# A graph network's edge rows: more of them fetched row by row by SyncE and ScalarE, fewer by GpSimd's gathers

## The reference

```python
x_src = x[src]; x_dst = x[dst]
e = relu((x_dst - x_src) @ theta_w.T + theta_b + x_src @ phi_w.T + phi_b)
x = layernorm(x + segment_max(e, dst))            # 0 for nodes without edges
hv = x @ W_in + b_in
for W, b in ((W_u0, b_u0), (W_u1, b_u1)):
    m = relu(concatenate([hv[src], edge_attr_64]) @ W + b)
    hv = where(has_in, segment_max(m, dst) + hv, hv)
x = layernorm(x + relu(hv @ W_ro + b_ro))
```

## Time and profile before

| | |
|---|---|
| device time, median of 3 runs | 4386.74 us |
| lowest and highest of the 3 | 4368.79 and 4420.99 us |
| span of the profiled execution (first to last instruction) | 3216.1 us |
| TensorE's mean granted clock in it | 0.922 |

### The profile page before, as it was taken

One profiled execution on the slowest core, in us unless ns is written; L12 is line 12 of the kernel. 1 busy time (PEld: TensorE's weight loads), 2 busy tenths in 40 slices (PEclk: granted clock), 3 DMA queues, 4 the chain that ended last, 5 costly groups with the idle time before them and its releaser, 6 DMA issues.

```text
span 3216.1 us, 33579 instructions
## 1 busy us (share of the span) xinstructions
PE 2494.2 (78%) x6386; PEld 1183.3 (37%) x6386; DVE 1457.3 (45%) x3424; ACT 196.1 (6%) x439; POOL 2359.0 (73%) x2484
## 2 busy tenths in 40 slices
PE   8776666666676888887887888688888888888877
PEld 6432222222223533333333333353333344333335
DVE  2675556555556533333433334323333343333337
ACT  2000000000002400000000000010000000000005
POOL 5777777777776677777777777667777777777765
PEclk9898888788877999999999999899999999999989
DMA  7666667666665777777777777687777777777764
GB/s 263 232 223 222 225 224 268 221 224 214 211 210 191 246 242 244 245 244 244 245 252 246 245 244 247 207 271 249 250 251 252 252 267 247 253 249 252 250 210 153
DMA packets 266593, 762.66 MB, mean 237 GB/s; under 512 B 57652, under 2 KB 113823, under 8 KB 229903
## 3 DMA queue, kind: packets, MB, share of 16 engines
q0 software_dynamic: 118896, 324.63, 33.2%
q1 hardware_dynamic: 94110, 356.95, 28.8%
q10 hardware_dynamic: 53376, 78.93, 7.9%
HBM read 413.88 MB, written 346.41 MB: 236 GB/s over the span
## 4 chain that ended last, share of the span: by engine, by line
POOL 39%; PE 17%; DMA 16%; issue 16%; SPq 7%; DVE 2%; ACT 2%; DVEq 0%; ACTq 0%; POOLq 0%
POOL gath L606 38%; DMA gath<-table,src_sb 14%; PE edge_ps L887 6%; SPq L530 4%; PE edge_ps L885 3%; PE edge_ps L778 3%; SPq L526 2%; PE side_ps L778 2%; PE edge_ps L864 2%; POOL gath L633 1%; DVE hist L410 1%; ACT x_sb L718 1%; DMA runs<-hist 1%; SPq L529 1%; DMA table<-hist 1%
## 5 line engine op out<-in xcount | busy, mean ns | idle before, releaser
L606 POOL DMA_INDIRECT gath<-table,src_sb x2288 | 2165.4, 946 | 745.0 <-issue 649.6
L410 DVE SCALAR_TENSOR_TENSOR hist<-hist,lift,edge_ps 128x256 f32<-128x256 f32 x2346 | 1127.0, 480 | 1564.3 <-PE edge_ps L887 1142.8
L887 PE MATMUL edge_ps<-gath,ident 128*128 128x512 f32 x1548 | 842.6, 627 | 328.0 <-DMA gath<-table,src_sb 326.4
L885 PE MATMUL edge_ps<-w_e,he_sb 128*128 128x512 f32 x1564 | 813.9, 602 | 5.5 <-DMA he_sb<-in_he 5.0
L864 PE MATMUL edge_ps<-gath,ident 128*128 128x512 f32 x740 | 476.3, 767 | 269.9 <-DMA gath<-table,src_sb 164.2
L887 PEld LDWEIGHTS edge_ps<-gath,ident 128*128 128x128 f32 x1548 | 275.7, 193 | 803.9 <-DMA gath<-table,src_sb 595.9
L885 PEld LDWEIGHTS edge_ps<-w_e,he_sb 128*128 128x128 f32 x1564 | 295.4, 194 | 352.7 <-issue 335.0
L864 PEld LDWEIGHTS edge_ps<-gath,ident 128*128 128x128 f32 x740 | 155.5, 236 | 532.5 <-DVE hist L410 317.1
L676 ACT COPY hv_sb<-side_ps 128x256 f32<-128x256 f32 x147 | 54.8, 373 | 2770.2 <-PE edge_ps L887 1842.9
L633 POOL DMA_INDIRECT gath<-runs,end_row x147 | 152.1, 1035 | 49.0 <-issue 43.6
L786 PE MATMUL edge_ps<-dst_f,onehot 128*128 128x512 f32 x200 | 78.0, 514 | 14.2 <-DVE onehot L333 14.2
(11 more groups left out here) (137 smaller groups left out, 1070.6 us busy)
## 6 DMA issues: line engine op xcount, KB each, us to landing
runs<-hist SPq DMA_DIRECT2D x285, 1024.0 KB, 5.0
he_sb<-in_he ACTq DMA_DIRECT2D x194, 256.0 KB, 2.9
late_sb<-table SPq DMA_DIRECT2D x3072, 1.0 KB
gath<-table,src_sb POOLq DMA_INDIRECT x2288, 3.4
table<-hist SPq DMA_DIRECT2D x72, 256.0 KB, 3.4
back_T<-x1T ACTq DMA_DIRECT2D x98, 128.0 KB, 3.2
runs<-hist SPq DMA_DIRECT2D x33, 256.0 KB, 2.9
x_sb<-in_x SPq DMA_DIRECT2D x49, 128.0 KB, 2.8
```

The costliest lines, as they stand in the source:

```text
L410: state = V.scalar_tensor_tensor(hist[:, s % H, :], hist[:, (s - 1) % H, :], lift[:, t:t + 1], edges, ALU.add, ALU.max)
L606: pool.indirect_dma_start(gath[:, s % G, :], None, a["x"] if s < RAW else tables[r], bass.IndirectOffsetOnAxis(src_sb[:, t:t + 1], 0)).the ...
L885: T.matmul(bank, he_sb[:, c % NHE, at:at + P], w_e[r - 1][:, :], start=True, stop=False)
L887: last = T.matmul(bank, ident[:, :], flat(edge_rows(s)), start=False, stop=True)
```

## The change

The number of row-by-row steps goes from 8 to 24 a round. SP fetches seven pairs of steps (first steps 120, 222, ..., 732): 14 steps, 1792 rows a round in place of 1024, 20 rows in each of the chunks 0 to 89. ACT fetches five pairs (first steps 148, 276, ..., 660): ten steps, 1280 rows a round, 16 rows in each of the chunks 0 to 79. POOL skips these 24 steps. The row numbers are multiplied by 1024 once, by DVE in the setup (12 small instructions), and written to `late_list` in HBM by one DMA after the 13th table write; the copies take the registers as byte offsets, so the instruction that computed an address falls away. [...] SP's destination is double buffered. ACT's is `he_sb` in round 0 (which is not in use there) and a part of `query_sb` afterwards, which joins the former `dst_f` and `junk`.

```diff
-LATE_AT = (360, 720)
-LATE = 4
-LATE_ROWS = 16
+LATE = 2
+LATE_PAIRS = 7
+LATE_EVERY, LATE_FIRST = 102, 120
+LATE_BUFS = 2
+LATE_PER_CHUNK = 20
+SIDE_PAIRS = 5
+SIDE_EVERY, SIDE_FIRST = 128, 148
+SIDE_PER_HALF_TURN = 16
+LATE_LOAD = 16
+ROW_BYTES = 4 * D
...
         def by_pool(t):
-            return t < STEPS and late_group(t) is None
+            return t < STEPS and late_pair(t) is None and side_pair(t) is None
...
             dve.wait_ge(edges_loaded, 16 * len(edge_loads))
+            firsts = [late_step(n) for n in range(LATE_PAIRS)] + [side_step(n) for n in range(SIDE_PAIRS)]
+            for n, first in enumerate(firsts):
+                last = V.tensor_scalar(late_at[:, n, :], src_sb[:, first:first + LATE], ROW_BYTES, None, ALU.mult)
+            reached("late offsets", last)
...
             def late_rows(r, c):
...
+                total = LATE_PAIRS * P * LATE
+                i, end = min(c * LATE_PER_CHUNK, total), min((c + 1) * LATE_PER_CHUNK, total)
+                while i < end:
+                    n, at = divmod(i, P * LATE)
+                    m = r * LATE_PAIRS + n
+                    count = min(LATE_LOAD, end - i, P * LATE - at)
...
+                    nc.sync.load(regs, late_list[n:n + 1, at:at + count])
+                    for k, reg in enumerate(regs):
+                        p, t = divmod(at + k, LATE)
+                        offset = nc.sync.snap(reg, donate=True, min_val=0, max_val=(NPAD - 1) * ROW_BYTES)
+                        sp.dma_start(late_sb[p:p + 1, m % LATE_BUFS, t, :].bitcast(mybir.dt.uint8),
+                                     table_bytes[r][bass.DynSlice(offset, ROW_BYTES)].rearrange("(o f) -> o f", o=1)
+                                     ).then_inc(late_landed[m], 16)
+                    i += count
...
             for u in range(NU):
                 write_table(0, u)
+                if u == LIST_UNIT:
+                    sp.wait_ge(setup_step, setup_at["late offsets"])
+                    with nc.allow_non_contiguous_dma("small layouts"):
+                        sp.dma_start(late_list.rearrange("n (p k) -> p n k", k=LATE), late_at[:, :, :]
+                                     ).then_inc(late_listed, 16)
...
                 for i in range(TURNS):
...
+                    for c in range(i * BODY // HC, (i + 1) * BODY // HC):
+                        if r > 0 and c + NHE < HE_CHUNKS:
+                            load_he(r, c + NHE)
+                        if c * HC % BODY == 0:
+                            for t in back_tiles(r, i):
+                                keep_back(r * TILES + t)
+                                if r > 0 and t + 2 < TILES:
+                                    load_back(r * TILES + t + 2)
+                        side_loads(r, c)
```

More of the change, by code:

```diff
@@ L99, in gnn_kernel @@
         ident = sb("ident", [P, P])
+        dst_f, junk = query_sb[:, 0:STEPS + 1], query_sb[:, STEPS + 1:]
+        above = junk[:, 0:P]
         col_no = sb("col_no", [P, P])
@@ L221, in groups_to, with late_step, late_pair, side_step @@
             return s // STRIDE * GROUPS + min(s % STRIDE // GS + 1, GROUPS)
-        def late_group(t):
-            return next((n for n, first in enumerate(LATE_AT) if first <= t < first + LATE), None)
+        def late_step(n):
+            return LATE_FIRST + n * LATE_EVERY
+        def late_pair(t):
+            n, k = divmod(t - LATE_FIRST, LATE_EVERY)
+            return n if 0 <= n < LATE_PAIRS and k < LATE else None
+        def side_step(n):
+            return SIDE_FIRST + n * SIDE_EVERY
+        def side_pair(t):
+            n, k = divmod(t - SIDE_FIRST, SIDE_EVERY)
+            return n if 0 <= n < SIDE_PAIRS and k < LATE else None
+        def side_rows(m):
+            at = m % LATE_BUFS * LATE * D
+            of = flat(he_sb[:, :, :]) if m < SIDE_PAIRS else query_sb
+            return of[:, at:at + LATE * D].rearrange("p (t f) -> p t f", f=D)
         def by_pool(t):
-            return t < STEPS and late_group(t) is None
+            return t < STEPS and late_pair(t) is None and side_pair(t) is None
         def pairs_in_slot(s):
@@ L509, in write_turned @@
                 sp.dma_start((x1T, msgT)[r][:, lo * D:hi * D], flat(turned(u))).then_inc(turned_written[u % UNIT_BUFS], 16)
-            late_regs = [nc.sync.alloc_register(f"late_reg{k}") for k in range(LATE_ROWS)]
             def late_rows(r, c):
[L514 to L531, removed]
@@ new lines, in late_rows @@
+                total = LATE_PAIRS * P * LATE
[4 more added lines that the diff above has]
+                    count = min(LATE_LOAD, end - i, P * LATE - at)
+                    if i == 0:
+                        for written, k in all_written(staged_written, r + 1):
+                            sp.wait_ge(written, k)
+                        sp.wait_ge(late_listed, 16)
+                    if at == 0 and m >= LATE_BUFS:
+                        was_r, was_n = divmod(m - LATE_BUFS, LATE_PAIRS)
+                        sp.wait_ge(group_summed, groups_to(was_r * STRIDE + late_step(was_n)))
+                    regs = [nc.sync.alloc_register(f"late{r}_{i + k}") for k in range(count)]
+                    nc.sync.load(regs, late_list[n:n + 1, at:at + count])
[6 more added lines that the diff above has]
+                    i += count
```

68 lines of the change are left out of this document (44 added, 24 removed).

## The result

| | kernel before | changed kernel |
|---|---|---|
| device time, median of 5 runs | 4399.77 us | 4730.02 us |
| lowest to highest | 4368.79 to 4457.42 | 4673.33 to 4737.1 |
| ratio, with its 95% interval | | 1.0717 [1.0653, 1.0782] |
| span and time of the profiled execution | 3216.1, not given | 4671.5, 4673.33 |

The change costs 7.2%. The profiled execution of the changed kernel takes 1.8 us more than its span, so there are no 1170.6 us outside the span. The kernel before has two levels, about 3217 us and about 4375 us, and the times of kernels that ran together are all of one level. The trace ahead of the prediction is of the lower level, while the times beside it, and the result above, are of the upper.

The account below looks back on a forecast made before the run. POOL was taken to bound the kernel before, SP the changed one. Rounds of +56, -7 and -11 us gave +38 on 4386.7, so 4425 us, +0.9%, with ACT at nothing; range 4322 to 4562 us.

Parts of the forecast that it names:

- 1170.6 us: Difference between the median time and the trace's span, taken as unchanged time outside the span; a change would upset the forecast.
- 0.338 us: SP's forecast price for issuing one row in the changed kernel: copy, its MOVE and pauses, without the address instruction.
- SP's part: SP's queue becomes the bound in chunks with rows: +56 us in round 0, -7 and -11 after, together +38 us.
- POOL's part: POOL loses 16 gathers a round at 1.25 us: 20.0 us a round, 60 us in all, if it still sets the pace.
- The small load: SP's second register load per chunk, of four numbers, taken as 0.7 us.
- the recovery behind the last row: Eight chunks without rows at the end of each round, taken as 45 us together.
- ACT's part: ACT's row copies, 7.7 us a chunk, about 8.5 with its other loads, against SP's 10.25; costed at nothing.
- `keep_back` stands at most one batch later: In ACT's queue, this copy is delayed by one batch of rows at most, while PE's next side product is 16 steps away.
- 232 against 232 us: Round 0: ACT's first pair is issued near 232 us; PE wants it at 227 plus 5 for landing, just in time.
- What hides it is SP's own lag: SP's slower chunks were to cover ACT's row work, so that ACT added 0 us.
- Rival 4: One transfer engine fills with all 36 row copies of a chunk: 9.9 us a chunk, -5 us, 4382 us; chance 0.04.
- Rivals 1 to 3: POOL still sets the pace, 4327 us, 0.32; dear register loads, 4806 us, 0.10 beyond +150; ACT late, 5290 us, 0.05.

Follow-up runs that it names:

- e19: The kernel before, unchanged, profiled at the upper level: 4377.42 us, ratio 1.0023 to the kernel before, span 4321.5 us.
- e8: The changed kernel, unchanged, against the kernel before at the lower level: 3378.17 us, ratio 1.0502; a second profiled execution at the upper level spans 4647.3 us.
- e10: Changed kernel with ACT's five pairs given back to POOL, repeated: ratio 1.0195 to the kernel before at the lower level; an upper-level execution spans 4477.6 us.
- e4: Changed kernel with SP's and ACT's row-by-row steps all given back to POOL: 3247.37 us, ratio 1.0089 to the kernel before, lower level.
- e17: Changed kernel with SP alone fetching rows, five pairs, 16 rows a chunk: 3211.21 us, ratio 0.9979 to the kernel before, lower level.
- e21: Changed kernel with 16 rows a chunk by SP and 8 by ACT: 3197.54 us, ratio 0.9934 to the kernel before, lower level.
- e2: Changed kernel with ACT's five pairs given back to POOL, SP's 20 rows a chunk alone: 3277.44 us, ratio 1.0193 to the kernel before, lower level.
- e3: Changed kernel with SP's seven pairs given back to POOL, ACT's rows alone: 3235.45 us, ratio 1.0054 to the kernel before, lower level.

## Why the prediction was wrong

**The time of the trace.** I took 1170.6 us as lying outside the span. They lay inside, in executions at the upper level that the trace didn't show. A sum made on the lower level's rows can't be added to the upper level's time: there SP's queue is the bound throughout in the changed kernel, its rests ahead of stores are under 20 us a round in the stretch with rows, and a row costs more than 0.338 us in every slow batch. This adds some 200 us to the loss (350 us between the spans of e19 and the result, 146 between those of before and e8). By the single spans at the upper level, SP's part costs 142 us there (before to e10) in place of my 38, and ACT's 170 (e10 to e8) in place of nothing. It is what I had named as upsetting all of it; I gave it no chance and no room in the range.

**POOL's part was right**: 1.1 to 1.3 us a gather in e4, e17 and e21, for 1.25. **SP's part was right at the lower level**, in direction and mechanism, and short in size: +57 to +60 us with SP alone for +38 forecast. Round 0 ended 51 us later for 56, but rounds 1 and 2 were 6 us longer and equally long, where I had taken off 7 and 11. The small load was 0.76 us for 0.7 (about +15 us in all), and the recovery behind the last row took 47 to 52 us for 45.

**ACT's part is the step that failed**: "I cost ACT at nothing". Its rows cost 18 us alone and 81 more beside SP's at the lower level, and some 170 us at the level of the result. "`keep_back` stands at most one batch later" holds once ACT keeps pace; at the start of round 0 it stands ten batches later, PE waits 25 us, and ACT alone costs 18 us. I had looked at whether the rows come in time, 232 against 232 us, and not at what stands behind them in the queue. "What hides it is SP's own lag" is the second error, since SP's stretch is the bound itself and a rest in it is added to it: SP rests 20 us longer in round 0 of e8 than of e2. The third is that ACT's copies were taken to leave SP's as they are: SP's stretch with rows grew by 90 us at the lower level and by 166 at the upper.

**Rival 4 had a mechanism that the lower level shows, and not its price.** It put 2.9 us of row copies beside 7.0 of other work and got 9.9 us a chunk, below SP's 10.25, so "less than SP's own bound". At 36 rows a chunk the last rows landed up to 21 us late where 16 us were at hand, the edge features in 15.5 in place of 2.9 us, and SP's own copies grew by 45 us. So here a backlog came, and cost time, though the work summed for the path stayed under SP's bound. How full it was is not shown: the price of 0.076 us was a mean over ACT's larger transfers, and in round 0 of e3, where ACT's queue moves rows alone, a row leaves a packet of 1 KB and one of 4 bytes, 0.052 and 0.009 us, which makes 2.2 us for 36 rows, as an estimate. At the level of the result the backlog isn't seen, so it doesn't explain the 7.2%.

That all row copies go through the same transfer engine is not shown either. Their semaphore records do show that a row copy isn't spread as a store is: 2 updates for each row copy in e2, 16 for each store to `runs`. The Trainium skill (DMA: Bandwidth & Descriptors, Why a DMA increments its semaphore by 16 and not by 1) says that software has to split a contiguous copy of a single dimension for it to be spread, and that a transfer which uses k engines on these queues uses the k lowest-numbered ones; a backlog over both queues that isn't there at 24 rows and is at 32 agrees with it.

**Rivals 1 to 3** fall: with SP's 20 rows stores stood over 10 us apart, the small load was not dear, and for ACT's rows alone PE waited 25 us in all, not hundreds. That the forecast had the sign right, slower, is in part luck: at the lower level SP's part would have given it, but what made most of the measured loss was not in the sum.

## What to carry to other kernels

Where a median and the span of the trace beside it differ by more than a few us, the trace shows another regime than the times: look for the bound that could grow between the two, and give the other regime a chance of its own. When work is put on a half-idle queue, price what stands behind it in program order in its worst phase, here the catch-up at a round's start, and not only the new work's own due time. A path that a sum fills nearly to the bound should be read as late landings for everything that shares it; 16 rows by SP and 8 by ACT, which left room on all three, was faster than 20 and 16, which freed POOL of more. And try the kernel with none of the added work, too, in the regime that the times are of: there no rows at all beat every split of them.

## What the runs showed of the hardware

- The same kernel takes 3217 or about 4375 us, at a mean granted TensorE clock of 0.92 or 0.80; the times of kernels that ran together share the level, and the same chip showed both. At the upper one SP issues 16 row copies in 6.4 us in one batch and in over 20 in another. The kernel with 16 and 8 rows gains more there (3.4% in place of 0.7%), and without rows the span is 3780.6 us in place of 4335.2.
- Row copies of 1 KB, one at a time, with other transfers beside them, at the lower level: 24 in about 10 us land within 4 us, 32 within about 20. A row copy leaves 2 updates of its semaphore, a store of 128 partitions 16.
- A register load of 4 numbers takes 0.76 us on SP, one of 16 takes 2.1 us; on ACT one of 16 takes 2.4 us (medians of e2 and e3).
